# Audio tower on one core: the six iterations of the pseudo-inverse written out instead of looped

## What is computed

```
def moore_penrose_iter_pinv(x, iters=6):
    z = jnp.swapaxes(x, -1, -2) / (jnp.max(col) * jnp.max(row))
    I = jnp.eye(x.shape[-1], dtype=x.dtype)
    for _ in range(iters):
        xz = x @ z
        z = 0.25 * z @ (13.0 * I - xz @ (15.0 * I - xz @ (7.0 * I - xz)))
    return z
...
out = attn1 @ (attn2_inv @ (attn3 @ v))
```

## Time and profile before

| | us |
|---|---|
| median of 3 runs | 964.54 |
| lowest, highest | 959.35, 964.63 |
| profiled execution | 964.83 |
| its span, first to last instruction | 963.10 |
| mean granted TensorE clock over the span | 0.896 of 2.4 GHz |
| PE, VectorE, ScalarE, GpSimd busy | 762.8, 612.2, 306.3, 214.3 |
| the six iterations, first to last instruction | about 675 to 806 |

### The profile page before, as it was taken

How to read it: one execution, slowest core, us unless ns; L and a number is a source line. 1 busy time by engine, 2 the same in 40 slices (tenths; PEclk the granted TensorE clock), 3 DMA queues, 4 the chain that set the end, 5 groups by cost and what they waited for, 6 DMA issues and landing times. The chain is left out here.

```text
span 963.1 us, 11862 instructions
## 1 busy us (share of the span) xinstructions
PE 762.8 (79%) x4033; PEld 560.7 (58%) x4033; DVE 612.2 (64%) x1445; ACT 306.3 (32%) x505; POOL 214.3 (22%) x253
## 2 busy tenths in 40 slices
PE   0069998899989998999998625728888886489987
PEld 0026665565546664565555424617788885389977
DVE  4918555784658555244645545899888889744377
ACT  0043334333532434333312120202232331236433
POOL 3000000000000000000000030653678778318401
PEclk9999998899979898899997556859899999889999
DMA  1350420016000320000000070000000000200000
GB/s 56 43 124 1 75 65 1 0 23 118 0 2 0 68 60 0 1 1 0 1 1 1 0 303 0 1 0 1 1 0 0 0 0 0 74 1 1 1 1 25
DMA packets 22554, 25.31 MB, mean 26 GB/s; under 512 B 17052, under 2 KB 21212, under 8 KB 21404
## 3 DMA queue, kind: packets, MB, share of 16 engines
q1 hardware_dynamic: 22508, 24.74, 10.7%
HBM read 21.05 MB, written 3.66 MB: 26 GB/s over the span
## 5 line engine op out<-in xcount | busy, mean ns | idle before, releaser
L565 PE MATMUL ps<-h,w 128*128 128x400 f32 x720 | 294.8, 554 | 1.1 <-ACT h L633 0.9
L565 PEld LDWEIGHTS ps<-h,w 128*128 128x128 f32 x720 | 141.4, 203 | 106.9 <-issue 104.4
L725 DVE COPY h<-ps 128x800 f32<-128x800 f32 (+2 forms) x58 | 56.6, 975 | 97.8 <-PE ps L565 97.1
L578 PEld LDWEIGHTS ps<-averager,sq 128*100 128x100 f32 (+2 forms) x1024 | 101.9, 175 | 22.3 <-ACT sq L626 18.5
L578 PE MATMUL ps<-averager,sq 128*100 128x1 f32 (+2 forms) x1024 | 102.4, 230 | 7.8 <-ACT sq L626 7.3
L626 ACT ACTIVATE sq<-h 128x800 f32<-128x800 f32 (+2 forms) x58 | 49.9, 860 | 179.1 <-DVE h L725 179.1
L1062 PE MATMUL pt<-for_pe,ident 128*128 128x156 f32 (+2 forms) x420 | 76.9, 348 | 35.3 <-DVE for_pe L1256 35.3
L1062 PEld LDWEIGHTS pt<-for_pe,ident 128*128 128x128 f32 x420 | 69.0, 219 | 42.6 <-DVE for_pe L1256 38.7
L633 ACT ACTIVATE h<-h,lnp 128x800 f32<-128x800 f32 (+2 forms) x58 | 60.6, 1045 | 84.6 <-DVE h L756 82.8
L756 DVE TENSOR_TENSOR h<-h,ps 128x400 f32<-128x400 f32 (+2 forms) x116 | 60.0, 559 | 39.3 <-PE ps L594 39.3
L605 ACT ACTIVATE h<-ps,lnp 128x800 f32<-128x800 f32 x64 | 63.4, 1011 | 64.1 <-PE ps L526 63.9
(11 more groups left out here) (269 smaller groups left out, 1131.7 us busy)
## 6 DMA issues: line engine op xcount, KB each, us to landing
late<-windows_dram SPq DMA_DIRECT2D x24, 375.0 KB, 7.5
gate_w<-in_gate_w SPq DMA_DIRECT2D x1, 3456.0 KB, 13.0
up_w<-in_up_w SPq DMA_DIRECT2D x1, 3456.0 KB, 19.3
windows_dram<-parts SPq DMA_DIRECT2D x12, 250.0 KB, 4.9
acts<-in_down_w SPq DMA_DIRECT2D x1, 1728.0 KB, 8.2
w<-in_w SPq DMA_DIRECT2D x1, 1024.0 KB, 5.7
xs<-in_x SPq DMA_DIRECT2D x4, 252.5 KB, 4.4
out_tokens<-hidden SPq DMA_DIRECT2D x6, 96.0 KB, 1.6
```

Of the source, the lines that this page charges most:

```text
L565: mm = pe.matmul(out, w[:, L.first_tap + t, :], source(l, s, 2 * p + c, t), start=(t == 0), stop=(t == L.taps - 1))
L578: mm = pe.matmul(var_ps[0:L.w, at:at + 1], sq[:, n["var"] % 2, c, q * L.w:(q + 1) * L.w], averager[:, 0:1], start=True, stop=True)
L725: nc.vector.tensor_copy(joined(l, s, p, r).rearrange("p (c b) t -> p c b t", c=2), ypair[n["bank"]][:, :, 0:L.cols].rearrange("p c (b t) - ...
```

## The change

The four loops become Python loops: the body stands six times in the program of each engine, and every count waited for is a constant. Nothing else differs; order, buffers and operations on each engine are the same.

```
@@ -1073,7 +1073,7 @@
                 pe.wait_ge(eye_ready, 5)
                 pe.matmul(pt[:, 3, 512:513], ones[:, :], top_norms[:, 2:3], start=True, stop=True).then_inc(scale_spread, 1)
                 sums(outer, at_outer)
-                with pe.Fori(0, PINV_ITERS) as n:
+                for n in range(PINV_ITERS):
                     sums(squaring, at_iteration(n))
                     sums(closing, at_iteration(n).after(squaring))
                 sums(applying, at_applying)
@@ -1130,7 +1130,7 @@
                 multiply(valuing, at_valuing)
                 multiply(outer, at_outer)
                 pool.wait_ge(e_ready, 1)
-                with pool.Fori(0, PINV_ITERS) as n:
+                for n in range(PINV_ITERS):
                     multiply(squaring, at_iteration(n))
                     pool.wait_ge(cubic_ready, n + 1)
                     multiply(closing, at_iteration(n).after(squaring))
@@ -1199,7 +1199,7 @@
                 copies(outer, at_outer)
                 act.wait_ge(e_ready, 1)
                 bring([bank(1)], FULL, FULL, e1)
-                with act.Fori(0, PINV_ITERS) as n:
+                for n in range(PINV_ITERS):
 
                     bring_rows(0, e1, at_iteration(n))
                     act.activation(lined(e34), lined(e1), ACT.Copy, scale=0.75).then_inc(share_ready, 1)
@@ -1348,7 +1348,7 @@
                     in1=eye[:, :, :].rearrange("p i j -> p (i j)").unsqueeze(1).broadcast_to([P, HL, R * R]),
                     op0=ALU.mult, op1=ALU.add).then_inc(e_ready, 1)
                 dve.wait_ge(e_ready, 1)
-                with dve.Fori(0, PINV_ITERS) as n:
+                for n in range(PINV_ITERS):
                     sums(squaring, at_iteration(n), NEAR0 + 2 * n, NEAR0 + 2 * n + 1)
                     dve.wait_ge(share_ready, n + 1)
                     nc.vector.scalar_tensor_tensor(out=lined(c4), in0=lined(e2), scalar=0.25, in1=lined(e34),
```

## The result

The changed kernel takes 956.88 us (median of 22 runs, 955.53 to 962.65), the kernel before 961.49 us (median of 22 runs, among them the three shown above). The ratio is 0.9954, with a 95% interval from 0.9938 to 0.9969: 4.4 us less, 3.0 to 6.0. Against the median of 22 runs the forecast effect of 0.5 us was too small by a factor of nine.

The account below looks back on a forecast made before the run. No engine was full; an iteration's path was almost all work, with 0.45 us of handovers in 20.96. Savings of 0.25 (back edges) and 0.24 (c4 waits) made -0.49 us, from 964.54 to 964.0 us; 8 in 10 range 958.5 to 969.0.

Parts of the forecast that it names:

- The back edge, 5 x 0.05 us: VectorE's first product after each of five loop branches: starts 0.03 instead of 0.08 us after ScalarE's rows, saving 0.25 us.
- The comparison with the end of the loop: Straight code behind the loop: the same line starts 0.03 us after the same kind of ScalarE copy, against 0.08.
- The `c4` wait, 6 x 0.04 us: VectorE's waits before c4 in six iterations: 0.13 us becomes 0.09 as in straight code, saving 0.24 us.
- GpSimd's waits, nothing: GpSimd's closing start after c4: up to 0.23 us earlier, but covered by PE's second batch, so no gain.
- Upper bound, 0.45 us per iteration: All handovers on an iteration's path vanish: 0.45 us in 20.96, 6 x 0.45 = 2.7 us at most.
- The code, nothing, with 29 and 28 packets: Instruction fetch for five more bodies: q8 and q14 packets rise from 23 and 23 to about 29 and 28, at no cost.
- Rival 3: Code comes late in the iterations: each packet stalls its engine 1.3 us, 14.3 us more, 978.3 us; chance 0.09.
- The clock: Slow PE batches in the iterations: direction unknown, only in the range; -4.70 us if both go, +1.68 per further closing hit.
- rival 1: Both slow PE batches in the iterations fall away: 4.7 us less, 959.3 us; chance 0.14.
- Rival 4: The back edge was VectorE's whole 1.16 us idle, gone five times, plus 0.24 of c4: 958.5 us; chance 0.04.
- The rule of the Trainium skill: Taken branches to targets outside the two blocks at hand must fetch; by it the five back edges would be what costs.
- The base: Whole kernel: the median of three runs before, 964.54 us, from which the forecast was taken.

Follow-up runs that it names:

- a3: The kernel before with the loops of PE, GpSimd and ScalarE written out and VectorE's kept; 964.10 us, ratio 1.0013 to the kernel before.
- a4: The changed kernel run again for a second trace, nothing altered; 958.03 us, ratio 0.9946 to the kernel before.
- e4: The changed kernel, a fourth trace to count slow batches; one, the first squaring, 6.70 us; 147.0 us from L1346 to L1359.
- c2: The changed kernel with six more PE fillers ahead of each closing and six once ahead of the iterations; 964.00 us, ratio 1.0012 to the kernel before.
- d1: The changed kernel with one useless 128x128 VectorE product at each of the five edges between iterations; 964.92 us, ratio 1.0023 to the kernel before.
- d2: The changed kernel with two useless VectorE products at each of the five edges between iterations; 982.84 us, ratio 1.0173 to the kernel before.
- c1: The kernel before with six more PE fillers ahead of each closing and six once ahead of the loop; 960.58 us, ratio 0.9975 to the kernel before.
- d4: c2 with PE fillers added ahead of the transposes of the attention's output (8) and the output projection (6); 959.10 us, ratio 0.9955 to the kernel before.

## Why the prediction was wrong

**The back edge, 5 x 0.05 us: the step that failed.** It measured 5 x 0.33 = 1.65 us. I wrote that of VectorE's idle of 1.16 us "1.08 of it had passed before ScalarE's rows were there at 720.51". That took the releaser named in the earlier trace rows, ScalarE's L1175, for the one that was waited for. The code says otherwise. The first product of pass `n` waits until `near_ready` is `NEAR0 + 2 * n`. The bringing before the loop makes it 7, and each pass adds two. The edge in the earlier trace rows leads to pass 2, so the count needed is 11, and this copy in the middle of pass 1 had made it that:

```profile
709.25 0.30 ACT L1175 COPY pt<-e 128x156 f32<-128x156 f32 x1
```

The copy at 720.21 makes it 12, which only the second pair of products needs. Rows 0 and 1 are read where PE summed them. So the wait in force was `copied`, met at 720.17, and VectorE was late by 0.42 us. The comparison with the end of the loop was of another wait: there `applying` does wait for the bringing. The clause "it may not branch before `copied` reaches its count" was right, and its price stood in the rows: 720.17 to 720.59.

**The `c4` wait, 6 x 0.04 us**: right, 0.13 became 0.09. **GpSimd's waits, nothing**: right; its `closing` starts 0.15 us earlier and nothing comes of it, and a3 shows it for ScalarE and PE as well. **Loop entry**: not costed, 0.08 us more. **Upper bound, 0.45 us per iteration**: 0.35 was measured, so it held, but by luck. It counted ScalarE's bringing as work on the path; with the 0.42 us from the last copy to the product in place of 0.04 and 0.08, the handovers add up to 0.75 us.

**The code, nothing, with 29 and 28 packets**: 28 and 25, ten of them between 695 and 800 us, and no "issue" idle on PE there. Rival 3 falls. I had bounded it by a stall in straight code that the iterations do not have.

**The clock, left out of the sum because its direction could not be said**: it belonged there. One slow batch fewer, as a rule -1.67 us, goes with the shorter period in every trace; rival 1, in which both fell away, came true by half. The trace of the kernel before could not show it; the two slow batches in it looked like luck. Two sentences beside it fail too. "The change leaves the idles as they are": PE's idle ahead of `squaring` went from 1.14 to 0.80 us with the shorter edge. And that the hit depends "not on its length": behind up to 1.46 us of idle no batch was slow. With both terms the sum is -1.8 - 1.67 = -3.5 us, and from `e1` to `attn` 145.7 us in five of the six traces at 20.60 us against 149.0 to 149.1 in four of the five at 20.95 says 3.3. The measured 4.4 (3.0 to 6.0) and, in a4, 5.2 (2.8 to 7.5) include it, so nothing beyond 3.3 is proven. Should the 1 us between 3.3 and 4.4 be real, it does not lie behind the attention: from `attn` to the end of the span it takes 140.3 to 140.5 us in both groups, and 138.7 in the one trace of each whose first `squaring` was slow (before, e4). The attention starts at 559.3 us on average in the five traces at 20.95 us (557.4 to 561.1) and at 558.2 in the six at 20.60 (556.8 to 560.0), which overlap too far to prove a difference.

**Rival 4** named the right place and the wrong size: the back edge was on the path, with 0.33 of the 1.16 us. That its 958.5 us lies nearer to the measured 956.88 than the forecast is luck; the slow batch makes up for a part of what it had too much. The rule of the Trainium skill beside it (Runtime: NRT & Kernel Launch, Instruction fetch mechanics) ties the cost of a branch to code that must be fetched. In this kernel no packet moved over the edges, and the way back to the head still cost VectorE 0.29 us. So the saving did not come from where the Trainium skill's rule puts it.

**The base**: 964.54 us was the median of three runs, 3 us above that of 22. On the base of 961.49 the same range would have reached down to 955.4 and held the time; the effect would have been too small all the same.

## What to carry to other kernels

In this kernel a loop cost time only on the engine that had to take the branch after the last thing it waited for. Putting that wait at the head of the loop (b1) or writing out that one engine (a2) brought almost all of the shorter period or all of it, and the other loops could stay. Before a releaser in a profile is believed, work out which count the wait needs and who reaches it: the last event in time need not be the one waited for. And where some batches run at the low clock, a shift of 0.3 us per iteration can be worth as much again in slow batches, in either direction, and fillers that help in one stage need not help the total (c2). Judge such a change by the stage's own windows in several traces, and then by the totals of many runs, not by one of each.

## What the runs showed of the hardware that I had not expected

- Going back to a loop's head on VectorE, with no packet of code moved: 0.29 us behind the last wait (0.42 against 0.13), of which 0.13 to 0.14 are a gap behind the taken branch; 0.46 us with twice the body (0.59 against 0.13), with a gap of 0.25 to 0.28.
- A VectorE product of two SBUF operands, 128x128, took 0.29 us where it started before GpSimd's product on SBUF (nine of nine in d1 and d2), and 1.39 to 1.65 us where it started during one (six of six), ending 0.14 to 0.16 us after it. The timeline of d1 over the one long product:

```profile
714.50 1.55 POOL L1124 TENSOR_TENSOR from_pool<-e 128x702 f32<-128x702 f32 x1 [3.02 <-ACT e L1164]
714.81 1.39 DVE L1361 TENSOR_TENSOR pad<-ident 128x128 f32<-128x128 f32 x1 [3.06 <-ACT e L1164]
```

- The same idle of 1.66 to 1.67 us stood ahead of an output projection of 4.14 us (after, c1) and of one of 7.56 us at a low clock (c2). With fillers just ahead of it (d4) it took 4.14 us, but that these fillers were the reason is not shown, since c1 has none.
